# Attention over a sliding window: 64-row array tiles side by side in place of block-diagonal operands

## The reference, cut to what matters

```python
def _L1_attn_ref(x, Wq, Wk, Wv, Wu, bu):
    EMB, HEADS, K = (64, 8, 32)
    scale = e ** 0.25
    xp = jnp.pad(x, ((0, 0), (k - 1, 0), (0, 0)))
    q = (x @ Wq.T).reshape(b, t, h, e) / scale
    kk = (xp @ Wk.T).reshape(b, tp, h, e) / scale
    v = (xp @ Wv.T).reshape(b, tp, h, e)
    idx = jnp.arange(t)[:, None] + jnp.arange(k)[None, :]
    kw = kk[:, idx]
    vw = v[:, idx]
    dot = jnp.einsum('bthe,btkhe->bthk', q, kw)
    attn = jax.nn.softmax(dot, axis=-1)
    out = jnp.einsum('bthk,btkhe->bthe', attn, vw)
    return out.reshape(b, t, h * e) @ Wu.T + bu
```

## Time and profile before

| | us |
|---|---|
| median of three runs | 897.4 (896.23 to 898.78) |
| the profiled execution | 889.64 |
| span in its profile | 887.6 |
| mean granted clock of TensorE | 0.86 of full speed |

### The profile page before, as it was taken

How to read it: one execution, slowest core, us unless ns; L and a number is a source line. 1 busy time by engine, 2 the same in 40 slices (tenths; PEclk the granted TensorE clock), 3 DMA queues, 4 the chain that set the end, 5 groups by cost and what they waited for, 6 DMA issues and landing times.

```text
span 887.6 us, 40461 instructions
## 1 busy us (share of the span) xinstructions
PE 728.3 (82%) x18746; PEld 567.3 (64%) x18746; DVE 484.3 (55%) x840; ACT 417.0 (47%) x830; POOL 161.4 (18%) x190
## 2 busy tenths in 40 slices
PE   6787877788767887778788656999999999999546
PEld 2355555566633455555566545999999999998433
DVE  0565554455604645446455564666666666666654
ACT  1665455554315554546544143445445445545442
POOL 7000000000030000000000153343443443341300
PEclk8889878866769798887976578999999999999669
DMA  5400000000004000000000170000000000000002
GB/s 171 82 4 5 4 4 5 5 4 4 5 6 81 4 5 4 4 4 4 5 4 4 29 193 1 1 2 1 0 0 0 0 0 0 0 0 0 0 1 96
DMA packets 7835, 16.58 MB, mean 19 GB/s; under 512 B 1982, under 2 KB 5950, under 8 KB 7286
## 3 DMA queue, kind: packets, MB, share of 16 engines
q1 hardware_dynamic: 7678, 14.21, 6.3%
HBM read 10.34 MB, written 3.87 MB: 16 GB/s over the span
## 4 chain that ended last, share of the span: by engine, by line
PE 76%; issue 10%; DVE 6%; ACT 5%; POOL 1%; DMA 1%; SPq 0%; DVEq 0%
PE banks L227 20%; PE banks L145 14%; PE banks L696 7%; PE banks L680 7%; PE banks L726 6%; PE banks L458 4%; PE banks L737 4%; PE banks L716 3%; PE banks L691 2%; PE banks L180 2%; PE banks L166 2%; PE banks L707 2%; ACT hx L273 1%; DVE norm_stats L629 1%; ACT hy L278 1%
## 5 line engine op out<-in xcount | busy, mean ns | idle before, releaser
L227 PE MATMUL banks<-s,y 32*64 32x96 f32 (+9 forms) x10752 | 191.1, 268 | 66.0 <-issue 65.9
L318 DVE TENSOR_TENSOR s<-hy,hx 128x384 f32<-128x384 f32 (+3 forms) x336 | 144.4, 476 | 183.4 <-PE banks L227 181.8
L227 PEld LDWEIGHTS banks<-s,y 32*64 32x64 f32 x10752 | 160.2, 154 | 109.9 <-issue 100.2
L145 PE MATMUL banks<-w_dc,tiled 64*32 64x192 f32 x3584 | 130.2, 412 | 20.3 <-issue 13.7
L268 ACT COPY y<-banks 128x384 f32<-128x384 f32 x192 | 81.8, 484 | 114.0 <-PE banks L145 114.0
L145 PEld LDWEIGHTS banks<-w_dc,tiled 64*32 64x32 f32 x3584 | 74.3, 131 | 53.8 <-issue 26.6
L794 ACT COPY hy<-banks 128x512 f32<-128x512 f32 x64 | 37.6, 588 | 116.7 <-PE banks L726 116.7
L278 ACT ACTIVATE hy<-banks 128x512 f32<-128x512 f32 (+2 forms) x144 | 72.9, 583 | 38.4 <-PE banks L180 38.3
L898 POOL TENSOR_TENSOR y<-y,stats 128x1024 f32<-128x1024 f32 x33 | 62.8, 1902 | 142.2 <-DVE stats L839 142.2
L273 ACT ACTIVATE hx<-banks 128x384 f32<-128x384 f32 x144 | 61.4, 505 | 31.8 <-PE banks L166 23.9
L680 PE MATMUL banks<-src,s 128*128 (+1 forms) x560 | 75.0, 279 | 1.1 <-ACT src L617 1.1
(11 more groups left out here) (137 smaller groups left out, 876.9 us busy)
## 6 DMA issues: line engine op xcount, KB each, us to landing
src<-in_x_dram SPq DMA_DIRECT2D x4, 578.0 KB, 5.5
y<-in_w_dram SPq DMA_DIRECT2D x1, 2080.0 KB
off<-in_w_dram SPq DMA_DIRECT2D x2, 1024.0 KB
out_dram<-tokens SPq DMA_DIRECT2D x4, 512.0 KB, 2.6
offsets_dram<-tokens SPq DMA_DIRECT2D x32, 54.0 KB
off<-offsets_dram SPq DMA_DIRECT2D x16, 108.0 KB
w_dc<-in_w_dc_dram SPq DMA_DIRECT2D x2, 288.0 KB, 6.0
y<-in_w_attn_dram SPq DMA_DIRECT2D x1, 512.0 KB, 4.9
```

The lines of the kernel that those rows point to most:

```text
L145: last = nc.tensor.matmul(m.ps[32 * j:32 * j + 32, FIRST_BANK + (count + g) % RING, (col % 2) * 192:(col % 2) * 192 + 192], m.tiled[rows, ...
L227: last = nc.tensor.matmul(out[:, r0:r0 + strip.n, first:first + width], m.y[32 * j:32 * j + 32, g, (s // 3) % 2 * Y_SLOTS + strip.slot, co ...
L318: nc.vector.tensor_tensor(dst, hy, hx[:, :, r0:r0 + strip.n, :], ALU.mult).then_inc(cv.s_ready, 1)
```

## The change

Queries take 64-row tiles, one for each image: weights are 64 rows (an image's channels) by 128 columns (one head of each group), and the two images' matmuls go to banks 0 and 1. Still 8 matmuls, of half the rows. Scores take 64-row tiles too, one for each head group: 16 matmuls in place of 8, each with 128 columns of queries as its weights and 64 columns of keys. A head group needs the keys of both images on its own partitions, so POOL copies each window three times: as it is (`at.window`, 128 by 160), and both halves into the other half's partitions (`at.swapped`, 64 by 160 twice). The mask's two matmuls use 32 rows each. Values take 64 by 64 tiles, four at a time: rows by the half of the keys, columns by head group, banks 5 and 6; 16 matmuls a block in place of 8. Keys are turned by 2 transposes in place of 4, and DVE copies them once. Scores are made three blocks ahead, queries four, keys two; the loop's body has four blocks, and the last four blocks stand behind the loop, without the work for blocks that don't exist. Waits ahead of `values` are placed before the last matmul of the step ahead (`carry`). Probabilities have four buffers.

PE's and ACT's part:

```diff
-TURN_AHEAD, SCORES_AHEAD, QUERIES_AHEAD = 1, 2, 3
+TURN_AHEAD, KEYS_AHEAD, SCORES_AHEAD, QUERIES_AHEAD = 1, 2, 3, 4
...
+BODY = 4
+TURNS = ALL_BLOCKS // BODY
+SPAN = WINDOW + P
+SLOTS_P = 4
...
 def attention_pe(nc, pe, m, at):
-    def queries(i, b, hg):
+    def queries(i, b, carry=None):
+        pe.wait_ge(at.windows_ready, i * BODY + b + 1)
         if b:
-            pe.wait_ge(at.g_ready, (i * BLOCKS + b - 1) * 2 + hg + 1)
-        first = WINDOW + b % BLOCKS * P
+            pe.wait_ge(at.g_ready, (i * BODY + b) * 2)
         for h in range(H4):
-            last = nc.tensor.matmul(m.ps[:, hg, h * P:(h + 1) * P], at.a_heads[:, hg * H4 + h, :],
-                                    at.xh[:, bass.ds(i + b // BLOCKS, 1), first:first + P], start=True, stop=True)
-        last.then_inc(at.g_in_psum, 1)
-    def scores(i, b):
-        pe.wait_ge(at.g_ready, (i * BLOCKS + b) * 2 + 2)
-        pe.wait_ge(at.pair_windows_ready, i * BLOCKS + b + 1)
+            for image in range(2):
+                rows = slice(C * image, C * image + C)
+                if carry is not None and (h, image) == (H4 - 1, 1):
+                    carry()
+                last = nc.tensor.matmul(m.ps[:, image, h * P:(h + 1) * P], at.a_heads[rows, h, :],
+                                        at.window[rows, b % 4, WINDOW:SPAN], start=True, stop=True)
+                if h == H4 - 1:
+                    last.then_inc(at.g_in_psum, 1)
+    def scores(i, b, carry=None):
+        pe.wait_ge(at.g_ready, (i * BODY + b) * 2 + 2)
+        pe.wait_ge(at.swapped_ready, (i * BODY + b) * 2 + 2)
         if b:
-            pe.wait_ge(at.shifted, i * BLOCKS + b)
-        for bank in range(2):
-            nc.tensor.matmul(m.ps[:, 2 + bank, :], m.identity16[:, :], m.mask[:, :], start=True, stop=False,
+            pe.wait_ge(at.shifted, i * BODY + b)
+        for hg in range(HG):
+            rows = slice(TQ * hg, TQ * hg + TQ)
+            nc.tensor.matmul(m.ps[:, 2 + hg, :], m.spread_q[rows, :], m.mask[rows, :], start=True, stop=False,
                              skip_group_check=True)
-        for j in range(TILES):
-            for hg in range(HG):
-                bank, first = divmod((j * HG + hg) * 2 * KEYS, BANK)
-                last = nc.tensor.matmul(m.ps[:, 2 + bank, first:first + 2 * KEYS], at.g[:, b % 2, hg, j, :],
-                                        at.pair_windows[:, b % 2, j, :, :], start=False, stop=True,
-                                        skip_group_check=True)
+        for image in range(2):
+            for j in range(TILES):
+                first = (image * TILES + j % 2 * 2 + j // 2) * KEYS
+                for hg in range(HG):
+                    rows = slice(C * hg, C * hg + C)
+                    keys = at.window if image == hg else at.swapped
+                    if carry is not None and (image, j, hg) == (1, TILES - 1, HG - 1):
+                        carry()
+                    last = nc.tensor.matmul(m.ps[:, 2 + hg, first:first + KEYS], at.g[rows, b % 2, image, j, :],
+                                            keys[rows, b % 4, j * TQ:j * TQ + KEYS], start=False, stop=True,
+                                            skip_group_check=True)
         last.then_inc(at.scores_in_psum, 1)
     def turn_keys(i, b):
         if b:
-            pe.wait_ge(at.xw_ready, (i * BLOCKS + b) * 2)
-        pe.wait_ge(at.windows_ready, i * BLOCKS + b + 1)
-        for j in range(TILES):
-            last = nc.tensor.transpose(m.ps[:, 5, j * P:(j + 1) * P], at.windows[:, b % 4, j, :], m.identity[:, :])
+            pe.wait_ge(at.xw_ready, i * BODY + b)
+        pe.wait_ge(at.windows_ready, i * BODY + b + 1)
+        if b >= KEYS_AHEAD:
+            pe.wait_ge(at.added, i * BODY + b)
+        for odd in range(2):
+            last = nc.tensor.transpose(m.ps[:, 7, (2 + odd) * P:(3 + odd) * P],
+                                       at.window[:, b % 4, odd * TQ:odd * TQ + P], m.identity[:, :])
         last.then_inc(at.xw_in_psum, 1)
...
-    def values(i, b, image):
-        pe.wait_ge(at.pt_ready, (i * BLOCKS + b) * 2 + image + 1)
+    def before_values(i, b, image):
+        pe.wait_ge(at.pt_ready, (i * BODY + b) * 2 + image + 1)
         if image == 0:
-            pe.wait_ge(at.xw_ready, (i * BLOCKS + b) * 2 + 2)
-        pe.wait_ge(at.z_ready, (i * BLOCKS + b) * 2 + image + 1)
-        for j in range(TILES):
-            last = nc.tensor.matmul(m.ps[:, 6, j * P:(j + 1) * P], at.xw[:, b % 2, image, j, :],
-                                    at.pt[:, image, j * P:(j + 1) * P], start=True, stop=True)
+            pe.wait_ge(at.xw_ready, i * BODY + b + 1)
+        pe.wait_ge(at.z_ready, (i * BODY + b) * 2 + image + 1)
+    def values(b, image):
+        for odd in range(2):
+            first = (image * 2 + odd) * P
+            for hg in range(HG):
+                k = odd * HG + hg
+                for late in range(2):
+                    rows = slice(KEYS * late, KEYS * late + KEYS)
+                    last = nc.tensor.matmul(m.ps[C * hg:C * hg + C, 5 + late, first:first + P],
+                                            at.xw[rows, b % 2, odd, C * image:C * image + C],
+                                            at.pt[rows, image, k * P:(k + 1) * P], start=True, stop=True,
+                                            skip_group_check=True)
         last.then_inc(at.z_in_psum, 1)
     def project_values(i, b):
-        pe.wait_ge(at.z_ready, (i * BLOCKS + b) * 2 + 3)
-        pe.wait_ge(at.added, i * BLOCKS + b + 1)
+        pe.wait_ge(at.z_ready, (i * BODY + b) * 2 + 3)
+        if not exists(i, b + KEYS_AHEAD):
+            pe.wait_ge(at.added, i * BODY + b + 2)
+            pe.wait_ge(at.xw_ready, ALL_BLOCKS)
         z = at.z[:, :, :].rearrange("p a (j h q) -> p a h j q", j=TILES, h=H4)
...
                                         skip_group_check=True)
         last.then_inc(at.projected, 1)
-    for hg in range(HG):
-        queries(0, 0, hg)
+    def body(i):
+        for b in range(BODY):
+            if exists(i, b + QUERIES_AHEAD):
+                queries(i, b + QUERIES_AHEAD, lambda: before_values(i, b, 0))
+            else:
+                before_values(i, b, 0)
+            values(b, 0)
+            if exists(i, b + TURN_AHEAD):
+                turn_probs(i, b + TURN_AHEAD, 0)
+            if exists(i, b + SCORES_AHEAD):
+                scores(i, b + SCORES_AHEAD, lambda: before_values(i, b, 1))
+            else:
+                before_values(i, b, 1)
+            values(b, 1)
+            if exists(i, b + TURN_AHEAD):
+                turn_probs(i, b + TURN_AHEAD, 1)
+            if exists(i, b + KEYS_AHEAD):
+                turn_keys(i, b + KEYS_AHEAD)
+            project_values(i, b)
...
-    with pe.Fori(0, PAIRS) as i:
-        for b in range(BLOCKS):
-            scores(i, b + SCORES_AHEAD)
-            values(i, b, 0)
-            turn_probs(i, b + TURN_AHEAD, 0)
-            queries(i, b + QUERIES_AHEAD, 0)
-            values(i, b, 1)
-            turn_probs(i, b + TURN_AHEAD, 1)
-            queries(i, b + QUERIES_AHEAD, 1)
-            turn_keys(i, b + TURN_AHEAD)
...
+    with pe.Fori(0, TURNS - 1) as i:
+        body(i)
+    body(TURNS - 1)
```

ACT's copy and order, DVE's keys and order (exponentials, sums and joins do what they did):

```diff
     def values(i, b, image):
         if image == 0:
-            act.wait_ge(at.projected, i * BLOCKS + b + 1)
-        act.wait_ge(at.z_in_psum, (i * BLOCKS + b) * 2 + image + 1)
-        nc.scalar.copy(at.z[:, image, :], m.ps[:, 6, :]).then_inc(at.z_ready, 1)
-    for hg in range(HG):
-        queries(0, 0, hg)
...
+    def body(i):
+        for b in range(BODY):
+            if exists(i, b + QUERIES_AHEAD):
+                queries(i, b + QUERIES_AHEAD)
+            values(i, b, 0)
+            if exists(i, b + TURN_AHEAD):
+                probs(i, b + TURN_AHEAD, 0)
+            values(i, b, 1)
+            if exists(i, b + TURN_AHEAD):
+                probs(i, b + TURN_AHEAD, 1)
+            if exists(i, b + SCORES_AHEAD):
+                exponentials(i, b + SCORES_AHEAD)
...
     def keys(i, b):
-        dve.wait_ge(at.xw_in_psum, i * BLOCKS + b + 1)
-        if b:
-            dve.wait_ge(at.projected, i * BLOCKS + b)
-        for hg in range(HG):
-            rows = slice(KEYS * hg, KEYS * hg + KEYS)
-            nc.vector.tensor_copy(at.xw[rows, b % 2, :, :, hg * C:(hg + 1) * C].rearrange("p a j c -> p j a c"),
-                                  m.ps[rows, 5, :].rearrange("p (j a c) -> p j a c", j=TILES, a=2)
-                                  ).then_inc(at.xw_ready, 1)
+        dve.wait_ge(at.xw_in_psum, i * BODY + b + 1)
+        if b >= KEYS_AHEAD:
+            dve.wait_ge(at.projected, i * BODY + b)
+        nc.vector.tensor_copy(at.xw[:, b % 2, :, :].rearrange("p o n -> p (o n)"), m.ps[:, 7, 2 * P:4 * P]
+                              ).then_inc(at.xw_ready, 1)
...
+    def body(i):
+        for b in range(BODY):
+            if exists(i, b + SCORES_AHEAD):
+                less_max(i, b + SCORES_AHEAD)
```

(32 more changed lines are left out.)

177 lines of the change are left out of this document (87 added, 90 removed).

## The result

The kernel before took 898.09 us beside it (median of 4 runs, 896.23 to 902.99), the changed one 850.08 (4 runs, 846.87 to 852.07). The ratio is 0.9454, with an interval of 0.9406 to 0.9502: faster by 5.5%, 48 us. Forecast were 844, in a range of 815 to 885. The profiled execution took 852.07 us, 37.6 less than that of before.

The account below looks back on a forecast made before the run. PE was taken to bound the attention loop. Blocks of 7.0 instead of 8.25 us save 40, the end 9.6, the start 3: 52.6 off 889.6 gives 837.0, scaled by 0.9% to 844 us, range 815 to 885.

Parts of the forecast that it names:

- The bound: Attention loop: PE alone bounds it, 8.25 us a block before, about 7.0 after, still busy nearly throughout.
- rival 1: Scores in the loop get cheaper too, loads hidden behind streaming: 0.93 us a block, 27 us more saved, 817; chance 12%.
- rival 2: Tile changes cost more (870), or PE's clock drops for a tenth of the loop (866); chance 18%.
- Queries and values at half their price: Loop on PE: 64-row tiles run side by side, so queries and values take 0.89 us each, was 1.78.
- Rivals 3: Two row groups can't load 128-column fp32 weights together: queries 1.78, scores 3.56, block 9.7 us, kernel 930; chance 6%.
- 4 (8.8): Tiles of one matmul's two records block each other; queries and values unchanged, block 8.8 us, kernel 900; chance 3%.
- Scores unchanged: Loop on PE: scores, bound by loading 128 weight columns, stay at 1.78 us a block.
- Eight changes at 0.14: Loop on PE: 8 tile-shape changes a block in place of 2; with longer loads 1.22 us, was 0.28.
- The other engines: Loop: DVE about 4.6, ACT 4.1, POOL 3.1 us a block, with no wait that would reach PE.
- The end: Last blocks: dropping unread work saves 12.6 us, less 3 for lost cover of ACT's copies, net 9.6.
- The start: Ahead of the loop: 3 us saved, between 0 and 5, by fewer query steps despite one more block there.
- From the sum to the median: Whole kernel: 837.0 us for the profiled execution, scaled by the 0.9% that the median lies above it, gives 844.

Follow-up runs that it names:

- mask64: The changed kernel with the mask's two matmuls on 64 rows each, the scores' tile shape, leaving 7 tile changes a block; 831.27 us, ratio 0.9292.
- six_changes: The changed kernel with the mask on 64 rows and queries moved next to mask and scores, leaving 6 tile changes a block; 834.44 us, ratio 0.9327.
- the fillers: The changed kernel plus 36 unread 128-row matmuls, 8 ahead of the first queries and 28 between the start's steps; 831.14 us, ratio 0.9313.
- ACT's order: The changed kernel with ACT's two copies of the first turned probabilities ahead of the third exponential instead of behind it; 845.68 us, ratio 0.9456.
- the kernel with both: The changed kernel with 64-row mask, queries next to scores, ACT's probabilities ahead of the third exponential, and 36 unread matmuls; 834.31 us, ratio 0.9287.
- eight fillers ahead: The changed kernel with only the eight unread matmuls ahead of the attention, none between its first steps; 851.85 us in one run.
- double_stream: The changed kernel with each score matmul streaming 128 columns of keys in place of 64, giving wrong scores; 851.53 us in one run.

## Why the prediction was right, point by point

- **The bound.** Right: PE is without gaps for 201 of 202 us in the loop, at full clock. Neither the cheaper scores of rival 1 nor the fall of the clock of rival 2 came about there.
- **Queries and values at half their price.** Right: 32 records of values in 2 x 0.60, 16 of queries in 1.09, changes of tile included. Rivals 3 (loads one after the other, 9.7 a block) and 4 (8.8) fall by the period of 6.95.
- **Scores unchanged.** Right, and the cause too, by the two kernels with fewer weights and more stream: 0.026 us for 32 columns of weights makes 0.052 for 64, where the prediction read 0.051. Rival 1 wanted 0.93 us; they take 1.83 in mask64, where a change stands behind them alone. The Trainium skill, "TensorEngine Tiling (Array Packing)", theoretical speedup, gives up to twice for any dimension of 64 or less. Queries and values come near it (1.09 and 1.20 us with the changes in them, for 1.78 each), scores don't, as their 128 columns of weights load no faster. One of the prediction's supports was misread: the earlier trace rows count every record that overlaps the window, not those that begin in it. The runs of records themselves are

```profile
336.38 0.52 PE L227 MATMUL banks<-s,y 32*64 32x24 f32 x34
470.63 1.15 PE L227 MATMUL banks<-s,y 32*64 32x16 f32 x64
```

  With the last record's length (0.22 and 0.28 us) taken off, each of the eight tiles gets its next record after about 70 ns at full clock and 110 at half, not 59 and 100. That is still well over the 21 and 42 ns that 24 columns stream, so the conclusion holds.
- **Eight changes at 0.14.** Right on average: 1.18 us against 1.22. Single ones aren't read so well: the steps exceed their price by 0.09 (mask, keys) to 0.20 (queries), and the second transposes by 0.06, though no change follows them. What an edit removed is surer: 0.20 by mask64, 0.30 with six_changes. By the Trainium skill's page just named, key properties, a change of the mode drains the engine; the gaps agree. With six of them the block is 6.65.
- **The other engines.** Right in the loop: DVE, ACT and POOL within 0.4 us a block of what was written, no wait of PE for them, the exchange could be tripled at no cost.
- **The end.** 10.4 us beyond 31 blocks against 9.6, but its make-up was only partly right. The wait for ACT's copies was put at 3 us and is 2.4, the sum of four waits in the last blocks, of which the last two are

```profile
780.21 0.67 PE L760 MATMUL banks<-hy 64*64 64x128 f32 x16 [0.85 <-ACT hy L840]
781.57 1.09 PE L775 MATMUL banks<-hy,y 128*64 128x128 f32 x16 [0.69 <-ACT hy L840]
```

  The same trimming in the kernel before was worth 6.2 us. About 3.3 of the remaining 4.2 would be work put ahead of the loop, by the sum above.
- **The start, mis-sized, and the only term outside its bounds.** It was put at -3 (0 to -5) and is +4.3 in the profiled execution. The step that failed is "one more block of scores and queries is now made there, while the chain waits for DVE". It took from the earlier trace rows that the first queries run at the low level, and reckoned nothing else there at it. At 3.68 us a block of scores, PE left little waiting time in which to hide more. Where the clock is up from start to end, with the fillers, the start is 27.79, or 3.5 under before, and the -3 would have held; in mask64's execution it is 31.26, which is no gain and no loss. Rival 2 had a fall of the clock, but put it into the loop, where none is, not into the start. Fillers that keep the clock up take 7.8 us off; ACT's order takes 1.9 off. Together that is more than the miss of 7.3, but in the kernel with both they don't add (29.26, where 25.9 would be the sum), and a part of the 7.8 is the execution's.
- **From the sum to the median.** The sum gave -52.6 on the profiled execution; outside the convolutions it shows -45.0: start 7.3 short, the stretch ahead of it 1.8 short, end 1.1 better, rest 0.3 better. The scaling by 0.9% assumed that both profiled executions lie alike to their medians. That of before was below its median (889.64 against 898.09 in the later runs), that of after above (852.07 against 850.08). That this mattered little is luck: the profiled pair is 7.6 us short of its sum, the measured 850.08 is 6 us above 844.

## What to carry to other kernels

Cut small tiles by what they load as well as what they stream. 64-row tiles side by side halve a step if streaming set it, and leave it alone if the weight columns did. Then count the changes of tile shape in a loop and put steps of one shape next to each other: here a change costs 0.15 us on average, and two fewer, on a block of 6.95, brought 0.30. Look at the clock of the prologue by itself, and in more than one execution, for a start at the low level leaves little of PE's idle time in which added work could hide.

## What the runs showed of the hardware that I had not expected

- PE's granted clock stood at 1.2 GHz for 44 us (526.9 to 571.3) although PE was busy for 22 of the 26 us from 545 to 571. It had idled before that, with 12 busy of the 18 us from 527 to 545. In the loop, with nearly the same tiles, it then stood at 2.4 GHz throughout. With eight fillers ahead it had risen (0.98) and fell again to 0.50 in a stretch with 9.14 of 10 us busy. In mask64 and double_stream it rose in mid-start with no filler. What exactly it follows stays open.
- More matmuls didn't cost time. With 36 whose results nobody reads, the ratio is 0.9313 where the changed kernel has 0.9454, 13 us of 898. Of that, 7.8 us are seen in the stretch where they stand, against an execution that was low there, and 3.5 against mask64's. As mask64 has 0.9292 without a filler, whole times don't show that the fillers are the cause. In the profiled executions the convolutions, ahead of the fillers, differ by more than all of this (495.8 against 510.8).
- A GpSimd copy across halves of the partitions, 64x160, takes 0.35 us, a plain one of 128x160 takes 0.32.
